# A two-layer graph network kernel on one core: how the border rows of its scatter stage are made, and when half 1 of its source-ordered groups runs

## The chip, the cores and the metric

The kernel is one program on one core of a Trainium2 chip. Its time is the device time of that core in microseconds (us); the median of three timed runs stands for it. PE is TensorE, DVE VectorE, ACT ScalarE, POOL GpSimd and SP SyncE, which here only issues DMAs.

## What is computed

Two graph layers over 6,250 nodes. Layer 0 has 100,000 edges, 16 attributes for each, and takes a maximum over the edges of each node; `row` is `src`, and the edges come sorted by `dst`:

```python
def _L0_gnn_ref(x, edge_attr, row, col, W_m1, b_m1, ...):
    msg_1 = x @ W_m1.T + b_m1               # 6250 x 96
    msg_2 = x @ W_m2.T + b_m2
    msg_e = edge_attr @ W_me.T + b_me       # one row for each edge
    msg = jax.nn.relu(msg_1[row] + msg_2[col] + msg_e)
    msg = jax.nn.relu(msg @ W_net.T + b_net)
    agg = jax.ops.segment_max(msg, row, num_segments=N_NODES)
    agg = jnp.where(jnp.isfinite(agg), agg, 0.0)
    out = x @ W_o1.T + b_o1 + (agg @ W_o2.T + b_o2)
    return out
...
    x = _layernorm(x + _L0_gnn_ref(x, edge_attr_16, src, dst, ...), axis=-1)
    x = _layernorm(x + _L1_gnn_ref(x, edge_attr_16, src, dst, ...), axis=-1)
```

Layer 1 is an edge network of two dense layers with a GELU over the same edges, a sum over them for each node, and a norm. The change leaves it as it is; it takes the second half of the time.

## The kernel before, in words

Nodes are cut in 49 blocks of 128 (`NB`) for `src` and in 56 blocks of 112 (`ND`) for `dst`. Edges are handled in groups of four chunks of 128.

**Block 1** (L582 to L783) ranks the edges by `src`: 49 groups of one-hot rows on DVE (`hist_onehots`) that PE sums up (`hist_counts`), `ranks_pe` and `ranks_dve` behind them. Beside them PE makes two tables from `x1T`, the transposed nodes: `m1` (for `src`, kept as three bf16 limbs: L751, `rest` L765, and ACT's copies L679) and `m2` (for `dst`, L756 and L687).

**Block 3** (L1227 on) starts with a prologue. Where a block of 112 nodes begins inside a chunk, its row has to be made of two blocks: `border_rows` (DVE L1403), `border_turn` (PE L1622), ACT's copy (L1761), and `later_block` (PE L1615, DVE L1411) form the table `more`, four blocks (a quad) at a time, 14 quads. All engines wait for its last row (`x_chain`). SP clears 16 pad blocks of `slots` and POOL 33 meanwhile.

Then come 200 steps (`C_STEPS`) with 196 groups in `dst` order, called "c": PE turns one-hot rows and counts (`turn`, `equal`, `count`), and `product` forms four chunks in PSUM (`ps_u`), out of `dstT` times `m2` (L1567) plus the row of `more` through a product with the identity (L1571). ACT copies the sum into `ring_u` (`rows`, L1698), DVE puts each edge's place in the order of `src` in `ring_p` (`put`, L1371; `advance`, L1337, is the running count before it), and POOL scatters each chunk with one indirect DMA (L1298), four for a group. It waits for `ring_p` and `ring_u`.

The groups in `src` order, called "d", are 222: 111 (`GS`) of half 1 and 111 of half 2. One takes `load_u` on SP, `pre_u` (L1582, L1590) and `net` (L1599) on PE, `first` (L1720) on ACT, `scan` (L1395) on DVE, `turn_top` (L1607) on PE, `rows_out_of` and `store` on ACT (L1726, L1730). From step 110 (`K0`) one d turn stands in each c step, 90 in all. The other 21 turns of half 1 and half 2 follow in a `pipeline` after the c steps; half 2's loads wait until all groups have landed (`groups_sent`). The turns up to 90 (`KS`) have one PSUM bank of each kind ("alone"), the later ones two. POOL, after its last scatter, loads `x1T` again (L1303), because `ring_u` lay over its place, waits for the stores of half 1 and issues 49 gathers (L1309), later 49 for half 2 (L1316).

The order inside a step is fixed by lists named `order`, one for each engine, with a lag for each stage; `hooks` are small works tied to a step (histogram groups `H8`, `MARKS`, `RANKS`, `TABLES`).

## Time and profile before

| | us |
|---|---|
| median of three runs | 3780.2 |
| the three runs | 3772.44, 3780.2, 3789.65 |
| the profiled execution | 3754.61 |
| its span | 3752.6 |
| busy: PE, DVE, ACT, POOL | 2743.1, 1925.6, 1120.7, 1692.6 |
| granted clock of PE, mean | 0.804 of full speed |

The span is cut in stretches by what runs: to 89.4 blocks 1 and 2, to 128 the prologue, to 966 steps with c alone, to 1660 steps with c and d, to 1816 the rest of half 1, the start of half 2 and the first gathers, to 2096 half 2; layer 1 follows. `issue` as a releaser means that the engine waited for nothing that the profile shows, `remote` that the semaphore of another engine came, with a long way between its event and the start. A group or line of the kernel is named by L and its number.

### The profile page before, as it was taken

The numbers are of one execution on the slowest core, as the hardware profiler recorded it, in microseconds if no ns is written. First come the engines' busy times: TensorE is split into PE (matmuls) and PEld (weight loads), VectorE is DVE, ScalarE is ACT, GpSimd is POOL, SyncE is SP. The second block draws the span as 40 slices with busy tenths as digits, with TensorE's granted clock in tenths as the row PEclk, the third lists the DMA queues.
The fourth block names the chain that finished last, engine by engine and source line by source line (L and its number), as shares of the span: only waits on it lengthen the run. The fifth ranks groups of instructions, "written<-read, shape, count | busy, mean of one in ns | idle before, by whom it ended". The sixth has DMA issues, their size and how long they took to land. (4 is left out here: it accounts for less than half of the span.)

```text
span 3752.6 us, 82895 instructions
## 1 busy us (share of the span) xinstructions
PE 2743.1 (73%) x22172; PEld 2390.7 (64%) x22173; DVE 1925.6 (51%) x8319; ACT 1120.7 (30%) x2463; POOL 1692.6 (45%) x1819
## 2 busy tenths in 40 slices
PE   7877777776888878886699756666666666676667
PEld 6766666666776667764466545665666666666667
DVE  6644544433555555555588733444444444444446
ACT  3222222222344444444466621111111111111114
POOL 1455544555545454443311135555455454545443
PEclk8677767777899999888799877777777777777778
DMA  6322223111333333356588311111111111111111
GB/s 190 79 72 71 71 70 87 37 40 33 84 97 96 93 92 97 92 153 159 142 201 200 85 41 38 36 36 37 34 36 36 35 38 35 36 34 37 34 33 35
DMA packets 575909, 276.48 MB, mean 74 GB/s; under 512 B 499504, under 2 KB 542826, under 8 KB 575546
## 3 DMA queue, kind: packets, MB, share of 16 engines
q1 hardware_dynamic: 225752, 107.85, 11.9%
q0 software_dynamic: 55104, 99.54, 9.7%
q10 hardware_dynamic: 294818, 66.10, 8.4%
q8 instruction: 129, 2.11, 0.2%
q14 instruction: 106, 0.87, 0.1%
HBM read 151.69 MB, written 127.59 MB: 74 GB/s over the span
## 5 line engine op out<-in xcount | busy, mean ns | idle before, releaser
L1298 POOL DMA_INDIRECT edge_in_src_order<-ring_u,ring_p x784 | 772.1, 985 | 782.1 <-issue 493.0
L1979 POOL DMA_INDIRECT a_rows<-src_table,idx x782 | 744.0, 951 | 744.4 <-DMA idx<-src_c 521.2
L2059 PE MATMUL ps_h<-a_rows,ident 128*128 x1664 | 325.8, 327 | 276.4 <-issue 275.7
L2059 PEld LDWEIGHTS ps_h<-a_rows,ident 128*128 128x128 f32 x1664 | 276.6, 235 | 311.3 <-issue 310.8
L2099 ACT ACTIVATE h<-ps_h 128x512 f32<-128x512 f32 x208 | 124.2, 597 | 1151.8 <-remote 812.3
L2028 DVE TENSOR_SCALAR ohd_f<-iota_b,dloc_c 128x128 f32<-128x128 bf16 x832 | 186.0, 292 | 509.9 <-remote 424.8
L2064 PE MATMUL ps_h<-bpart,dstT_b 128*128 x1664 | 317.2, 351 | 171.5 <-ACT dstT_b L2093 137.0
L2064 PEld LDWEIGHTS ps_h<-bpart,dstT_b 128*128 128x128 f32 x1664 | 278.1, 253 | 202.0 <-issue 201.8
L1395 DVE TENSOR_TENSOR_SCAN top<-same,top,bank 96x512 f32<-96x512 bf16 x221 | 281.6, 1274 | 174.5 <-remote 109.0
L1337 DVE TENSOR_TENSOR prior<-bank,earlier 128x512 f16<-128x512 f32 x196 | 134.8, 688 | 454.6 <-remote 369.1
L2016 DVE TENSOR_TENSOR hsumT<-hsumT,ps_s 128x128 f32 x832 | 239.3, 288 | 191.1 <-issue 83.5
L1567 PEld LDWEIGHTS bank<-m,dstT 128*128 128x128 f32 x1568 | 240.8, 226 | 98.8 <-issue 96.7
L1599 PE MATMUL bank<-msg,wnet_s 97*96 97x512 f32 x444 | 252.8, 649 | 67.6 <-issue 41.3
L2073 PE MATMUL ps_s<-ohd_f,h 128*128 128x128 f32 x1664 | 283.2, 325 | 19.8 <-issue 14.6
L1567 PE MATMUL bank<-m,dstT 128*128 x1568 | 259.3, 313 | 35.5 <-issue 25.3
L2073 PEld LDWEIGHTS ps_s<-ohd_f,h 128*128 128x128 f32 x1664 | 266.5, 242 | 22.8 <-issue 18.8
L1571 PE MATMUL bank<-more,ident 128*128 x1568 | 251.5, 309 | 15.4 <-issue 13.2
L1571 PEld LDWEIGHTS bank<-more,ident 128*128 128x128 f32 x1568 | 227.9, 222 | 24.8 <-issue 22.9
L1590 PE MATMUL bank<-oh_b,m_s 128*96 128x128 bf16 x2664 | 203.7, 227 | 44.5 <-issue 37.6
L1720 ACT ACTIVATE msg<-bank,bias_c 96x512 f32<-96x512 f32 x222 | 151.2, 681 | 251.6 <-remote 235.6
L1590 PEld LDWEIGHTS bank<-oh_b,m_s 128*96 128x96 bf16 x2664 | 188.8, 129 | 48.2 <-issue 39.8
L1714 ACT COPY m_s<-m 128x288 bf16 x444 | 169.8, 430 | 159.7 <-PE bank L1590 104.2
(347 smaller groups left out, 5104.4 us busy)
## 6 DMA issues: line engine op xcount, KB each, us to landing
u_in<-edge_in_src_order SPq DMA_DIRECT2D x222, 192.0 KB
running_max<-row ACTq DMA_DIRECT2D x222, 192.0 KB
rowt<-src_row SPq DMA_DIRECT2D x222, 130.0 KB
running_max<-zero_rows ACTq DMA_DIRECT2D x37, 576.0 KB
key_b<-dst_of_edges ACTq DMA_DIRECT2D x832, 0.5 KB
edge_in_src_order<-ring_u,ring_p POOLq DMA_INDIRECT x784
a_rows<-src_table,idx POOLq DMA_INDIRECT x782
dge_attributes_by_column<-in_edge_attrT SPq DMA_DIRECT2D x8, 784.0 KB, 12.1
```

Source lines behind the costliest of these rows:

```text
L1298: pool.indirect_dma_start(u_d, bass.IndirectOffsetOnAxis(ring_p[:, j:j + 1], 0), ring_u[:, j, :], None).then_inc(sent[i % 4], 16)
L1395: v.tensor_tensor_scan(top[:, u % 2, :], same[:, u, :], pick_bank(ps_net, i, u), 0.0 if first else top[:, (u - 1) % 2, 4 * P - 1:4 * P], A ...
L1567: m.matmul(ps_u[:, j, :], dstT[:, u, j, :], m2[:, bass.ds(at[j], F)], start=(j == 0), stop=False, skip_group_check=True)
L1571: mm = m.matmul(ps_u[:, j, :], ident[:], more[:, bass.ds(of[j], F)], start=False, stop=True, skip_group_check=True)
L1590: mm = m.matmul(to[:, P * j:P * j + P], m1_s[:, u % 2, j, F * k:F * k + F], oh[:, u % 2, P * j:P * j + P], start=False, stop=(k == 2), ski ...
L1599: m.matmul(pick_bank(ps_net, i, u), wnet_s[:], msg[:, u % 2, :], start=True, stop=True).then_inc(net_ready, 1)
L1979: pool.indirect_dma_start(a_rows[:, 4 * u + j, :], None, a_d, bass.IndirectOffsetOnAxis(idx[:, u % 4, j:j + 1], 0)).then_inc(got[u % 4], 16)
L2016: adds.add(v.tensor_tensor(at, at, ps_s[k][:, j, :], ALU.add))
L2028: last = v.tensor_scalar(ohd[:, u, j, :], iota_b[:], dloc[:, u, j:j + 1], None, ALU.is_equal)
L2059: m.matmul(ps_h[k][:, j, :], ident[:], a_rows[:].rearrange("p c d -> p (c d)")[:, bass.ds(slot[j], D)], start=(j == 0), stop=False, skip_g ...
L2064: mm = m.matmul(ps_h[k][:, j, :], dstT[:, k, j, :], bpart[:, bass.ds(at[j], D)], start=False, stop=True, skip_group_check=True)
L2073: mm = m.matmul(ps_s[k][:, j, :], h[:, u, j, :], ohd[:, u, j, :], start=True, stop=True)
```

## The change

- `x1T` gets a place of its own, so the ten DMAs of L1303 are gone. The index inputs of block 1 lie in `agg_all` instead.
- Block 1 no longer makes `m1`. It makes the border rows instead: DVE `border_dve`, PE `border_pick`, DVE `border_local`, and then 14 quads of `border_rows`, of which POOL takes nine (36 instructions) and DVE five (19), with `border_turn` on PE and `border_copy` on ACT. PE waits for all of these copies before `ranks_pe`.
- Block 3 has no prologue. The quads' products and joins (`border_product`, `border_join`) stand in the hooks of steps 0, 1 and 2 (5, 5 and 4 quads); the histogram groups start one step later; `m1` is made in the hooks of steps 7 to 36 through PSUM bank 6.
- In `product` the four products with the identity are gone. ACT writes the rows of `more` into `ps_u` first (`seed`, lag 2, between `rows` and `rows_out_of`), and PE's four products add to them. `product` waits for `seeded`, and `seed` for `u_ready`.
- SP clears 20 pad blocks and POOL 29.
- All 111 turns of half 1 stand in the 90 steps from `K0` on (`in_turns`): 21 steps have a second d turn, behind everything else of the step. `KS` is 112. SP waits for `groups_sent` and then the 111 turns of half 2 follow.

```diff
+                def turn_of_half_1(now):
+                    return max(0, now - K0) * GS // (C_STEPS - K0)
+                def in_turns(order, now):
+                    ds = range(turn_of_half_1(now), turn_of_half_1(now + 1))
+                    for kind, lag, work in order:
+                        if kind == "c":
+                            step([(kind, lag, work)], "c", CG, now)
+                        elif ds:
+                            step([(kind, lag, work)], "d", GB, ds[0])
+                    for t in ds[1:]:
+                        for kind, lag, work in order:
+                            step([(kind, lag, work)], "d", GB, t)
...
-                KS = C_STEPS - K0 + 1 & -2
+                KS = GS + 1 & -2
...
                         def product(i, u, n):
                             pe.wait_ge(rec_in[u], 16 * (n + 1))
-                            wait(pe, u_ready, i)
+                            pe.wait_ge(seeded, i + 2)
                             at = offsets(nc, mybir.EngineType.PE, pf_row[:, 4 * i:4 * i + 4], ND * F - F)
                             for j in range(4):
-                                m.matmul(ps_u[:, j, :], dstT[:, u, j, :], m2[:, bass.ds(at[j], F)],
-                                         start=(j == 0), stop=False, skip_group_check=True)
-                            of = offsets(nc, mybir.EngineType.PE, xs_row[:, 4 * i:4 * i + 4], ND * F - F)
-                            for j in range(4):
-                                mm = m.matmul(ps_u[:, j, :], ident[:], more[:, bass.ds(of[j], F)],
-                                              start=False, stop=True, skip_group_check=True)
+                                mm = m.matmul(ps_u[:, j, :], dstT[:, u, j, :], m2[:, bass.ds(at[j], F)],
+                                              start=False, stop=(j == 3), skip_group_check=True)
                             mm.then_inc(sum_ready, 1)
...
+                        def seed(i, u, n):
+                            act.wait_ge(x_chain, ND)
+                            act.wait_ge(seeded, i + 1)
+                            wait(act, u_ready, i)
+                            at = offsets(nc, mybir.EngineType.Activation, xs_row[:, 4 * i:4 * i + 4], ND * F - F)
+                            for j in range(4):
+                                last = s.copy(ps_u[:, j, :], more[:, bass.ds(at[j], F)])
+                            last.then_inc(seeded, 1)
...
-                        for lo in range(0, NP, 5 * P):
-                            hi = min(lo + 5 * P, NP)
-                            g.dma_start(x1T[:, lo:hi], xT[:, lo:hi]).then_inc(x_back, 16)
```

On PE, in a step with one c group and one d turn near the middle of the stage, the c part of before stands so (`bank<-m,dstT` is L1567, `bank<-more,ident` L1571; `TENSOR_LOAD` and `ISA` fetch the four offsets):

```order
3822 L79 TENSOR_LOAD rows_b
3823 L1567 ISA
3824 L1567 MATMUL bank<-m,dstT 128x96
...
3830 L1567 MATMUL bank<-m,dstT 128x96
3831 L79 TENSOR_LOAD rows_b
3832 L1571 ISA
3833 L1571 MATMUL bank<-more,ident 128x96
...
3839 L1571 MATMUL bank<-more,ident 128x96
3840 L1536 MATMUL bank<-ohlo_a,prior 128x64 x4
```

And so after the change, on PE in a step with two d turns; L1632 is `net`, L1640 `turn_top`, L1615 and L1623 `pre_u`, L1566 the last of `equal`:

```order
3281 L1632 MATMUL bank<-msg,wnet_s 96x512
3282 L79 TENSOR_LOAD rows_b
...
3290 L1604 MATMUL bank<-m,dstT 128x96
3291 L1640 MATMUL bank<-ident,top 128x96 x4
3292 L1573 MATMUL bank<-ohlo_a,prior 128x64 x4
...
3300 L1566 MATMUL bank<-hiT 128x128 x4
3301 L1615 MATMUL bank<-ident,u_in 96x128 x4
3302 L1623 MATMUL bank<-oh_b,m_s 96x128 x12
3303 L1632 MATMUL bank<-msg,wnet_s 96x512
3304 L1640 MATMUL bank<-ident,top 128x96 x4
3305 L1615 MATMUL bank<-ident,u_in 96x128 x4
3306 L1623 MATMUL bank<-oh_b,m_s 96x128 x12
```

The identity products are gone, and `net`, `turn_top` and `pre_u` of the second turn stand in a row behind the step.

On ACT, in a step with one d turn, before:

```order
711 L1708 CAST dstT<-bank 112x512
712 L1698 COPY ring_u<-bank 128x384
713 L1726 COPY row<-bank 128x384
714 L1730 DMA running_max<-row 128x4x96
```

and after:

```order
1858 L1758 CAST dstT<-bank 112x512
1859 L1748 COPY ring_u<-bank 128x384
1860 L79 TENSOR_LOAD rows_b
1861 L1735 ISA
1862 L1735 COPY bank<-more 128x96
...
1868 L1735 COPY bank<-more 128x96
1869 L1776 COPY row<-bank 128x384
1870 L1780 DMA running_max<-row 128x4x96
```

`seed` (L1735) stands between the copy of the finished sum and the copy of the d turn's rows.

On DVE, in a step with two d turns, after the change (L1428 is `put`, L1452 `scan`, L1394 `advance`, which before stood right behind the one scan and L1355):

```order
2802 L1428 SCALAR_TENSOR_TENSOR ring_p<-across,spare 128x4
...
2813 L1452 SCALAR_TENSOR_TENSOR top<-same,top,bank 96x512
2814 L1441 TENSOR_SCALAR oh_b<-rowt,node_c 128x512
2815 L1443 TENSOR_TENSOR same<-rowt 96x512
...
2821 L1452 SCALAR_TENSOR_TENSOR top<-same,top,bank 96x512
2822 L1412 TENSOR_TENSOR rank_r<-rank_r,new 100x64
2823 L1394 TENSOR_TENSOR prior<-bank,earlier 128x512
```

The second turn's one-hot, copies and scan moved in ahead of the next group's `advance`.

## Rows read from the trace of the kernel before

**Rows 1.** Windows of all engines: stretch, then busy time, clock, DMA.

```profile
24.00:71.00 47.00, 47.00 (x551) 42.27 (x551) 35.97 (x94) 22.12 (x40) 0.00 (x0) 0.95 0.89 243
89.40:128.00 38.60, 34.84 (x179) 33.27 (x179) 27.82 (x120) 8.10 (x14) 18.23 (x34) 0.50 0.26 64
128.00:970.00 842.00, 622.57 (x5830) 544.31 (x5830) 386.79 (x2163) 218.40 (x471) 432.32 (x439) 0.77 0.25 63
970.00:1660.00 690.00, 563.48 (x5808) 477.94 (x5807) 391.83 (x1774) 299.12 (x670) 335.93 (x341) 0.90 0.36 95
1750.00:1816.00 66.00, 10.26 (x46) 5.96 (x44) 4.87 (x11) 2.82 (x6) 43.52 (x47) 0.54 0.21 47
```

The columns are the stretch, its length, then busy time and records of PE, PEld (weight load), DVE, ACT and POOL, and last the granted clock, the DMA share and GB/s.

**Rows 2.** The page's costliest groups: scatters and the two products.

```profile
L1298 POOL DMA_INDIRECT edge_in_src_order<-ring_u,ring_p x784 | 772.1, 985 | 782.1 <-issue 493.0
L1567 PE MATMUL bank<-m,dstT 128*128 x1568 | 259.3, 313 | 35.5 <-issue 25.3
L1571 PE MATMUL bank<-more,ident 128*128 x1568 | 251.5, 309 | 15.4 <-issue 13.2
```

**Rows 3.** Windows of the copy into ring_u (L1698), one per c step.

```profile
138.00:966.00 828.00, 53.25 (x110) 0.77 0.24 62
966.00:1661.00 695.00, 41.30 (x86) 0.90 0.36 95
```

**Rows 4.** Windows of the scan (L1395), one for each d turn.

```profile
966.00:1661.00 695.00, 109.01 (x86) 0.90 0.36 95
1680.00:1745.00 65.00, 31.36 (x25) 1.00 0.85 227
1745.00:1816.00 71.00, 4.56 (x5) 0.57 0.26 58
1816.00:2094.00 278.00, 130.82 (x103) 0.99 0.79 197
```

**Rows 5.** Timeline of DVE, the first and fifth scan after the c steps.

```profile
1660.20 1.28 DVE L1395 TENSOR_TENSOR_SCAN top<-same,top,bank 96x512 f32<-96x512 bf16 x1 [0.60 <-remote]
...
1677.51 1.28 DVE L1395 TENSOR_TENSOR_SCAN top<-same,top,bank 96x512 f32<-96x512 bf16 x1 [1.05 <-PE bank L1607]
```

A row of the timeline has start, duration, engine, line, operation, and in brackets the idle time before it with what released it.

**Rows 6.** Timeline around one burst of scatters, c alone: POOL, PE, ACT.

```profile
865.74 0.96 POOL L1298 DMA_INDIRECT edge_in_src_order<-ring_u,ring_p  x1 [0.31 <-issue]
870.94 0.96 POOL L1298 DMA_INDIRECT edge_in_src_order<-ring_u,ring_p  x1 [4.24 <-DVE ring_p L1371]
...
859.66 1.13 PE L1571 MATMUL bank<-more,ident 128*128 x8
870.02 1.91 PE L1571 MATMUL bank<-more,ident 128*128 x8
...
866.93 0.48 ACT L1698 COPY ring_u<-bank 128x384 f32<-128x384 f32 x1 [7.73 <-remote]
```

**Rows 7.** Timeline of one step with c and d: POOL, then DVE.

```profile
1123.74 0.96 POOL L1298 DMA_INDIRECT edge_in_src_order<-ring_u,ring_p  x1 [0.30 <-issue]
1127.27 1.07 POOL L1298 DMA_INDIRECT edge_in_src_order<-ring_u,ring_p  x1 [2.57 <-issue]
...
1124.89 0.69 DVE L1337 TENSOR_TENSOR prior<-bank,earlier 128x512 f16<-128x512 f32 x1 [2.78 <-remote]
1126.31 0.15 DVE L1371 SCALAR_TENSOR_TENSOR ring_p<-across,spare 128x4 int32<-128x4 f32 x1
```

**Rows 8.** Timeline of the prologue: a quad's products, its joins, the first scatter.

```profile
116.80 1.97 PE L1615 MATMUL bank<-m,dstT_x 112*128 112x96 f32 x8
...
123.33 1.36 DVE L1411 SCALAR_TENSOR_TENSOR more<-more,joint,bank 128x96 f32<-128x96 f32 x4 [0.42 <-PE bank L1615]
...
141.94 1.05 POOL L1298 DMA_INDIRECT edge_in_src_order<-ring_u,ring_p  x1 [28.31 <-DVE ring_p L1371]
```

**Rows 9.** Timeline of DVE in block 1, beside a cast of POOL.

```profile
12.72 0.79 DVE L431 TENSOR_SCALAR cmp_r<-bounds_r,dst_f 128x128 f32<-128x128 f32 x1
```

**Rows 10.** Timeline of POOL: the first gather of half 1.

```profile
1745.27 1.00 POOL L1309 DMA_INDIRECT agg_all<-running_max,last_i  x1 [69.38 <-SPq L1252]
```

More of the change, by code:

```diff
@@ L308, in gnn @@
         rec_moved = sem(whole, "rec_moved")
-        x_back = sem(whole, "x_back")
         agg_in = [sem(whole, f"agg_in{k}") for k in range(4)]
@@ L313, in gnn @@
         wo1_set = sem(whole, "wo1_set")
+        x1T = sb(whole, "x1T", [D, NP])
         with ExitStack() as t:
@@ L664, in _ @@
                             g.tensor_copy(dst_c[:], dst_ci[:]).then_inc(dstc_set, 1)
+                            for q in range(BY):
+                                border_rows(pool, g, q, 0)
                         @block.scalar
@@ L998, in _ @@
                                 chunks_dve(dve, v, ch, k0, bank[1])
+                                border_dve(dve, v, 1, bank[1])
+                                border_local(dve, v, 1, bank[1])
+                                for q in range(BX):
+                                    border_rows(dve, v, q, 1)
                                 dve.wait_ge(k0.off_set, 2)
@@ L1051, in _ @@
                                 chunks_act(act, nc.scalar, k0, bank[4:6], bank[6:8])
+                                for q in range(BX):
+                                    border_copy(act, nc.scalar, q, 1, bank[2:4])
                                 ranks_act(act, nc.scalar, c0, 0, bank[3])
@@ L1506, in _ @@
                         for now in range(C_STEPS):
-                            for kind, lag, work in order:
-                                step([(kind, lag, work)], kind, CG if kind == "c" else GB, now - (0 if kind == "c" else K0))
+                            in_turns(order, now)
                             hooks(now)
-                        pipeline(dve, GB, [(lag, work) for kind, lag, work in order if kind == "d"], done=C_STEPS - K0, early=KS + 4)
+                        pipeline(dve, GB, [(lag, work) for kind, lag, work in order if kind == "d"], done=GS, early=KS + 4)
                         groups_sent(dve, CG)
@@ L1754, in hooks @@
                             if now == K0 - 1:
+                                act.wait_ge(m_taken, 3 * NT)
                                 act.wait_ge(apart, 1)
-                        order = [("d", 2, first), ("c", 1, turned), ("c", 3, rows), ("d", 5, rows_out_of), ("d", 6, store), ("d", 0, stage)]
-                        for q in range(BX):
-                            act.wait_ge(x_turned, q + 1)
-                            wait(act, x_ready, q - 1)
-                            k = min(4, ND - 1 - 4 * q)
-                            s.copy(dstT_x[:, q % 2, 0:k].rearrange("p j e -> p (j e)"), ps_split[q % 2][0:BD, 0:P * k]).then_inc(x_copied, 1)
-                        act.wait_ge(x_chain, ND)
+                        order = [("d", 2, first), ("c", 1, turned), ("c", 3, rows), ("c", 2, seed), ("d", 5, rows_out_of), ("d", 6, store), ("d", 0, stage)]
                         for now in range(C_STEPS):
-                            for kind, lag, work in order:
-                                step([(kind, lag, work)], kind, CG if kind == "c" else GB, now - (0 if kind == "c" else K0))
+                            in_turns(order, now)
                             hooks(now)
                         act.wait_ge(rows_cleared, 16 * ZEROS)
-                        pipeline(act, GB, [(lag, work) for kind, lag, work in order if kind == "d"], done=C_STEPS - K0, early=KS + 4)
+                        pipeline(act, GB, [(lag, work) for kind, lag, work in order if kind == "d"], done=GS, early=KS + 4)
                         for k in range(4):
```

345 lines of the change are left out of this document (182 added, 163 removed).

## The prediction

> **What bounds the kernel now.** I read the windows first, then the costliest groups, then the timeline at one place of each stretch. The windows [rows 1] show PE busy for 622.57 of 842 us with c alone and for 563.48 of 690 us with c and d; POOL is at half in both. PE looks like the bound, and the change takes work from PE. The timeline says otherwise. POOL issues a scatter of 0.985 us with 0.30 between [rows 2, 6], so a group is four times 1.27, about 5.1 us. While such a burst runs, a semaphore from PE reaches the others late: the identity products started at 859.66 and took 1.13, but ACT copied their sum only at 866.93, after 7.73 us idle with releaser `remote`, just as the last scatter of the burst (865.74 + 0.96) was over [rows 6]. POOL then waited 4.24 us for `ring_p` of DVE. With c and d the same loop is regular [rows 7]: the last scatter ends at 1124.70, DVE's `advance` starts at 1124.89 after 2.78 us `remote`, `put` at 1126.31, the next group at 1127.27. That is 5.1 us of burst plus 2.57 of a chain through DVE and POOL, in which PE's products have no part. The strongest evidence is the copy into `ring_u` [rows 3]: 828 us for 110 steps is 7.53 a step with c alone; with c and d 90 steps take 695 us, 7.7 a step, though each has a whole d turn more on PE. A d turn costs PE, by half 2 where nothing else runs, about 2.5 us (257 busy in 278 us for 103 turns would be that; the 278 us themselves are 2.70 a turn [rows 4]). So 2.5 us more on PE moved the step by 0.17 to 0.2.
>
> **The change part by part**, against the profiled 3754.61 us.
>
> *Start of the scatters.* The first starts at 141.94 [rows 8]. The prologue of 38.6 us [rows 1] goes; the products of 14 quads (1.97 us each while PE is at 0.50 of its clock, the lower level of 1.2 GHz) and their joins (1.36 us) [rows 8] come back inside steps 0 to 2, and every `seed` waits for the last join. That is 14 x 1.36 = 19 us if DVE paces them, 14 x 1.97 = 28 if a cold PE does; I take 21, since the two overlap and PE comes out of less idle time. Block 1: from 24 to 71 us PE was busy for 47.00 of 47 us and DVE for 35.97 [rows 1]. Without the three limbs of `m1` DVE sets the pace, at most 11 us less, but it takes 19 row instructions and the border sums itself, and PE waits for the border copies before the ranks. I take 3.5 and keep 0 and 11. Sum: -38.5 + 21 - 3.5 = **-21**, bounds -11 and -30. POOL's share of the clears shrinks from 33 to 29 and is done before then, so it costs nothing; its cover is some 10 us thick.
>
> POOL's nine quads in block 1 run beside DVE's one-hot rows. The nearest row is a DVE instruction of 128x128 f32 beside a cast of POOL, 0.79 us [rows 9]; 36 of POOL's instructions at that length are 28 us, in some 45 us of histogram, so they are hidden at no loss. The Trainium skill, "SBUF — State Buffer", section "Who interferes with whom", speaks against this part: a DVE instruction with two inputs in SBUF, as the one-hot rows are, contends with one of GpSimd that reads SBUF, through a pair of ports that one of them holds for the whole instruction. By it the one-hot rows would wait for POOL and the 3.5 us would turn into a loss of some 3 to 10; no row of this case settles it.
>
> *Steps with c alone (110).* PE loses the identity products, 251.5 us in 196 steps [rows 2], 1.28 a step (8 records; 1.13 warm, 1.91 cold [rows 6]) and one fetch of offsets. If a step were PE's, that would be all gain: -140. If the loop of burst and late semaphore holds, the slope above, 0.2 in 2.5, gives 0.1 a step: -11. I take 0.18 a step, **-20**, because with c alone PE is cold more often and is sometimes late by itself; that is near the slope, for it is measured on the same loop. Bounds 0 and -90. ACT gets four copies a step and a fetch. One copy of all four blocks is 0.48 us [rows 6], so they cost between 0.48 and 4 x 0.48 = 1.9. ACT is busy for 218.40 of 842 us [rows 1]: hidden in time. What stands in the chain is new: `rows` then `seed` then `product`, where `product` waited for `rows` alone. The next product needs it one step later, and a step is 7.5 us against 2.4, so no one waits for it.
>
> *Steps with c and d (90).* The same products and copies, at the slope: 90 x 0.08 = **-7**, bounds +20 and -60 (ACT is busy for 299.12 of 690 [rows 1] and gets up to 171 us more, 68%). Making `m1` in the hooks puts 20 us on PE and 30 copies on ACT over 30 steps; beside a 2 us wait for the burst in each, nothing.
>
> *The second d turn in 21 steps.* It stands behind the step's other work on each engine; on DVE its scan goes ahead of the next `advance`, the instruction that releases the next burst. In one bank a turn costs 4.3 us by itself (1660.20 to 1677.51 is four turns [rows 5]). DVE waits 2.78 us for the burst anyway [rows 7], and PE 0 to 1. If all of it falls in there, the price is the slope's 0.25 a turn, +5; if nothing, 4.3, +90. I take the middle, 2.1 a turn: **+44**. The middle, because its inputs cross between PE and ACT twice, and with POOL in its burst a crossing is late, while half of its work fits.
>
> *The tail.* 21 turns no longer stand between the last scatter and the gathers. They ran at 2.6 us a turn (25 in 65 us [rows 4]), the first at 4.3; 21 x 2.7 = **-57**. What half 2 does meanwhile is not lost: from 1660 to 1745 it had begun with 8 turns, and it still has 111 to do at 2.70 [rows 4]. SP's wait for `groups_sent` now stops an empty pipeline: last landing, load, three lags, **+8**, bounds 5 and 20. The 49 gathers come 66 us of near standstill as before (PE 10.26 of 66 us [rows 1], 5 scans in 71 us [rows 4]), wherever they fall. POOL had waited 69.38 us before the first gather [rows 10], so its ten loads of `x1T` were hidden and their absence is worth 0.
>
> Sum: -21 - 20 - 7 + 44 - 57 + 8 = **-53**, so 3702 against 3754.6. The median of the shown runs is 3780.2, 25.6 above the profiled run; the prediction is 3780.2 - 53 = **3727**.
>
> **The rivals.**
> *PE is the bound after all.* For it: busy 74 and 82% [rows 1]. Against: rows 3 and 7. Half of what the product lost in 196 steps would be -125 in place of -27, so -151: 3629. All of it: 3504. Chance 0.17.
> *The second turn takes the place of DVE's slack.* Slower. If the second scan of a step starts after the burst is over, `advance`, `put` and the next burst come later by the whole turn: +90 for 44. With it the products give nothing (0 for -27) and the empty pipeline costs 20 for 8: -21 + 90 - 57 + 20 = +32, 3812. It decides from the point where a second turn's inputs arrive more than 2.8 us after the first scan. For it: the crossings. Against: rows 7, where the wait of 2.78 is longer than the scan's 1.3. Chance 0.15.
> *A colder clock.* PE's granted clock is 0.77 with c alone and 0.90 where it has more to do; it is 0.54 where it is idle [rows 1], and eight products take 1.9 us in place of 1.1 [rows 6]. With less work PE may be at 1.2 GHz more often: if one step in three that is now warm turns cold, 37 x 0.8 = +29, and the -20 is gone, -53 + 49 = -4: 3776. Chance 0.16. The Trainium skill, "TensorE: Matmul & The Clock Gate", section "HAM oscillation — how this bites in real kernels", says that gaps between bursts of matmuls put the clock back to half, each time anew. The trace agrees (0.77 in a stretch full of gaps); the page would give this rival, since the gaps grow by what the product loses.
>
> **How the numbers follow.** The sum has 0.52, the others as above. Its own range is 3680 to 3765 by the bounds of the double steps and of the c steps. The range of 8 in 10 leaves out the far end of the first rival (about 0.1) and the slower rival's far end (0.08): 3645 to 3795. A measurement of this kernel tells about 0.5% from no change, 19 us. Faster by more: 0.50 of the sum, all of the first rival, little of the clock: 0.68. Within: 0.17, mostly the clock. Slower: 0.15.
>
> **What would show it.** The first scatter near 121 us; a c step at 7.35 us and a c and d step at 7.6, with double steps near 9.8 (the copies into `ring_u` in windows); `advance` still released by `remote` at the end of a burst; the first gather at 1745.27 - 21 - 20 - 7 + 44 - 57 + 8, near 1692 us, with some 8 turns of half 2 before it, and half 2 at 2.70 a turn. I am wrong if the c step falls below 7 us (PE was the bound), if double steps take over 12 us, if the first scatter comes after 130, or if the granted clock with c alone is under 0.7.

## The result and the profile after

The changed kernel takes 3732.4 us (median of four runs, 3724.6 to 3745.5) and the kernel before 3779.0 us (four runs, 3772.4 to 3789.7): a ratio of 0.9883, 95% interval 0.9857 to 0.9908. The forecast was 3727.

The windows of the changed kernel, with the same columns as [rows 1]: block 1, the start of block 3, c alone, c and d, the first gathers, half 2.

```profile
24.00:71.00 47.00, 43.17 (x505) 37.94 (x505) 42.44 (x117) 13.30 (x24) 33.56 (x36) 1.00 0.94 260
...
86.00:124.00 38.00, 30.44 (x205) 28.50 (x206) 27.38 (x100) 6.59 (x19) 16.04 (x30) 0.63 0.44 101
124.00:960.00 836.00, 549.13 (x4957) 463.94 (x4955) 376.24 (x2120) 306.96 (x924) 431.11 (x440) 0.70 0.24 61
960.00:1684.00 724.00, 552.75 (x5589) 448.56 (x5590) 432.23 (x1874) 396.03 (x1092) 345.25 (x340) 0.87 0.40 105
...
1710.00:1800.00 90.00, 32.05 (x233) 22.57 (x231) 23.95 (x52) 18.35 (x41) 48.33 (x51) 0.64 0.37 88
1800.00:2072.00 272.00, 249.22 (x2171) 180.19 (x2170) 220.46 (x489) 174.75 (x395) 44.63 (x47) 1.00 0.80 196
```

With c alone PE is busy for 549 of 836 us, where it was 623 of 842 [rows 1], and its granted clock is 0.70 instead of 0.77. ACT has gone from 218 to 307 us. The stretch has not become shorter. That is best seen at the copies into `ring_u`: their 1st, 110th, 111th and last in the changed kernel, and then the same four in the kernel before.

```profile
120.77 0.48 ACT L1748 COPY ring_u<-bank 128x384 f32<-128x384 f32 x1 [1.24 <-PE bank L1604]
...
953.07 0.50 ACT L1748 COPY ring_u<-bank 128x384 f32<-128x384 f32 x1
959.33 0.48 ACT L1748 COPY ring_u<-bank 128x384 f32<-128x384 f32 x1 [1.12 <-remote]
...
1683.97 0.48 ACT L1748 COPY ring_u<-bank 128x384 f32<-128x384 f32 x1 [6.47 <-remote]
```

```profile
138.69 0.48 ACT L1698 COPY ring_u<-bank 128x384 f32<-128x384 f32 x1 [2.04 <-PE bank L1571]
...
960.91 0.48 ACT L1698 COPY ring_u<-bank 128x384 f32<-128x384 f32 x1 [1.81 <-PE bank L1571]
967.14 0.49 ACT L1698 COPY ring_u<-bank 128x384 f32<-128x384 f32 x1
...
1659.97 0.48 ACT L1698 COPY ring_u<-bank 128x384 f32<-128x384 f32 x1 [0.91 <-remote]
```

So the start is 17.9 us earlier; 109 steps with c alone take 832.3 us for 822.2, 10.1 longer; 85 steps with c and d take 724.6 for 692.8, 31.8 longer, with 20-odd second turns in them. What comes after that is shorter: half 2's last two scans (one row of the view) start 386.4 us behind the last copy, where they started 432.9 behind it. These four add up to -22.5 us, and the spans differ by 20.6 (3732.0 and 3752.6). The medians differ by 46.6, because the profiled run of before was 24 us under its median; so no single stretch of this pair may be read closer than some 20 us.

The experiments ran on four chips, and the table below can't be read without that. On two (here A1 and A2) the kernel before takes 3727 us, 1.4% under the recorded 3779; on two others (B1, B2) the same program takes 2661 and 2663 us. Each chip was used in one session only, so what is called a kind of chip below may also be a state in which the chips were found.

### The profile page after: what moved, and what is told of

Same layout as the page of the kernel before. It is cut to its first block and busy times, and to the rows that moved or that the text cites. A ratio compares the mean times of both kernels' runs of the same rounds, so it can differ in the third digit from the quotient of the medians.

```text
span 3732.0 us, 80433 instructions
## 1 busy us (share of the span) xinstructions
PE 2598.2 (70%) x20605; PEld 2232.4 (60%) x20606; DVE 1919.0 (51%) x8284; ACT 1261.5 (34%) x3246; POOL 1721.3 (46%) x1841
## 5 line engine op out<-in xcount | busy, mean ns | idle before, releaser
L1359 POOL DMA_INDIRECT edge_in_src_order<-ring_u,ring_p x784 | 780.2, 995 | 800.6 <-issue 549.2
L2105 PEld LDWEIGHTS ps_h<-a_rows,ident 128*128 128x128 f32 x1664 | 278.4, 237 | 324.8 <-issue 324.0
L1452 DVE TENSOR_TENSOR_SCAN top<-same,top,bank 96x512 f32<-96x512 bf16 x221 | 281.0, 1272 | 147.0 <-remote 88.7
L1604 PEld LDWEIGHTS bank<-m,dstT 128*128 128x128 f32 x1568 | 263.9, 244 | 148.8 <-issue 147.7
L1604 PE MATMUL bank<-m,dstT 128*128 x1568 | 283.1, 332 | 76.1 <-issue 57.2
L1394 DVE TENSOR_TENSOR prior<-bank,earlier 128x512 f16<-128x512 f32 x196 | 134.7, 687 | 377.6 <-remote 340.5
L1632 PE MATMUL bank<-msg,wnet_s 97*96 97x512 f32 x444 | 266.3, 680 | 71.7 <-DVE top L1452 35.8
L1623 PE MATMUL bank<-oh_b,m_s 128*96 128x128 bf16 x2664 | 210.6, 229 | 67.7 <-issue 67.6
L1623 PEld LDWEIGHTS bank<-oh_b,m_s 128*96 128x96 bf16 x2664 | 192.6, 131 | 77.8 <-issue 76.4
L1770 ACT ACTIVATE msg<-bank,bias_c 96x512 f32<-96x512 f32 x222 | 151.0, 680 | 160.7 <-remote 122.9
L1735 ACT COPY bank<-more 128x96 f32 x784 | 148.8, 237 | 129.7 <-ACT ring_u L1748 83.7
L1615 PE MATMUL bank<-ident,u_in 128*96 128x128 f32 x888 | 144.4, 286 | 41.6 <-ACT msg L1770 34.3
```

The source lines that it names most:

```text
L1359: pool.indirect_dma_start(u_d, bass.IndirectOffsetOnAxis(ring_p[:, j:j + 1], 0), ring_u[:, j, :], None).then_inc(sent[i % 4], 16)
L1452: v.tensor_tensor_scan(top[:, u % 2, :], same[:, u, :], pick_bank(ps_net, i, u), 0.0 if first else top[:, (u - 1) % 2, 4 * P - 1:4 * P], A ...
L1604: mm = m.matmul(ps_u[:, j, :], dstT[:, u, j, :], m2[:, bass.ds(at[j], F)], start=False, stop=(j == 3), skip_group_check=True)
L1623: mm = m.matmul(to[:, P * j:P * j + P], m1_s[:, u % 2, j, F * k:F * k + F], oh[:, u % 2, P * j:P * j + P], start=False, stop=(k == 2), ski ...
L1632: m.matmul(pick_bank(ps_net, i, u), wnet_s[:], msg[:, u % 2, :], start=True, stop=True).then_inc(net_ready, 1)
L2105: m.matmul(ps_h[k][:, j, :], ident[:], a_rows[:].rearrange("p c d -> p (c d)")[:, bass.ds(slot[j], D)], start=(j == 0), stop=False, skip_g ...
```

## The experiments

Every kernel here, the controls too, waits in three places of the gathers and of layer 1 against a loaded value masked with `& 255`, which changes none of the values. All edits are against the changed kernel, but for r1. "Against before" is the ratio to the kernel before on the same chip. The stretches are from the profiled run, as the copies into `ring_u` mark them. The code of the c steps is the same in the recorded changed kernel, r3 and e5, and with c alone in e2 too: their stretches lie between 810.0 and 832.3 us with c alone and between 707.1 and 724.6 with c and d, which shows how closely one trace may be read.

| run | chip | median us | against before (95%) | 1st copy at | c alone, 109 steps | c and d, 85 steps | last copy to half 2's last two scans |
|---|---|---|---|---|---|---|---|
| before (recorded) | - | 3779.0 | 1 | 138.7 | 822.2 | 692.8 | 432.9 |
| after (recorded) | - | 3732.4 | 0.9883 (0.9857 to 0.9908) | 120.8 | 832.3 | 724.6 | 386.4 |
| r3 after | A2 | 3689.3 | 0.9909 (0.9884 to 0.9935) | 123.1 | 813.8 | 719.1 | 383.4 |
| e8 products back | A2 | 3723.4 | 0.9996 (0.9973 to 1.0019) | 120.2 | 817.7 | 748.5 | 384.2 |
| e3 longer burst | A2 | 3532.3, one run | - | 120.6 | 712.9 | 661.6 | 387.4 |
| e6 split burst | A2 | 3633.0, one run | - | 120.6 | 771.3 | 700.2 | 389.3 |
| e2 one turn a step | A1 | 3682.1 | 0.9874 (0.9852 to 0.9897) | 120.5 | 817.2 | 658.7 | 436.8 |
| e5 gathers in pairs | A1 | 3626.4 | 0.9731 (0.9709 to 0.9753) | 120.5 | 810.0 | 707.1 | 322.9 |
| r1 before | B1 | 2662.4, one run | - | 138.5 | 524.0 | 466.1 | 373.6 |
| r2 after | B1 | 2659.7 | 0.9994 (0.9980 to 1.0009) | 121.9 | 524.1 | 536.6 | 324.8 |
| e1 products back | B1 | 2643.6 | 0.9934 (0.9918 to 0.9951) | 120.1 | 525.9 | 514.3 | 326.6 |
| e4 no border rows | B1 | 2605.3 | 0.9786 (0.9770 to 0.9802) | 120.5 | 523.5 | 450.4 | 354.7 |
| c1 pairs, DMA in mid | B2 | 2824.2 | 1.0608 (1.0590 to 1.0627) | 120.9 | 557.9 | 526.8 | 336.6 |
| c2 pairs, DMA at end | B2 | 3250.2 | 1.2211 (1.2191 to 1.2232) | 120.0 | 555.7 | 535.6 | 327.4 |

**The kernel before, once more.**

> The kernel before once more, for a second trace of it. The profiled run of before (3754.6 us) lay 24 us under the median of its timed runs (3779.0), while that of after (3733.8) lay on its own (3732.4). If that was chance, this trace shows a time near 3779, and the 20 to 25 us sit in the c steps (the copies into ring_u took 822.2 us from the first to the 110th, and 692.8 from the 111th to the last); the start (138.7), the tail and layer 1 should repeat within 3 us. If timed runs are always slower than a profiled one, this trace repeats 3755 within 5.

It ran on a chip of the second kind, and neither expectation fits: 2662 us. With that it became the most telling of all runs, since the kernel is the same. What DVE waited for in the steps with c alone (line and operand, releaser, us in total, times, longest), first in the recorded trace from 200 to 900 us, then here from 200 to 600:

```profile
DVE prior L1337 <- remote: 185.8, 34, 9.2
DVE prior L1337 <- PE bank L1529: 64.8, 18, 6.8
```

```profile
DVE prior L1337 <- PE bank L1529: 60.9, 58, 4.4
```

In the recorded trace 31 of these 34 releases come during the last scatter of a run or up to 1.9 us behind it. (`remote` has to be read with care: the semaphore's event stands right before the start, and what is long is the way to it from the end of PE's instruction. In [rows 6] the products ended at 860.79 and the copy began at 866.93.) On B1 the late semaphores are gone, and POOL goes from group to group without a break, here over a border of two groups:

```profile
602.28 0.96 POOL L1298 DMA_INDIRECT edge_in_src_order<-ring_u,ring_p  x1 [0.31 <-issue]
603.54 0.96 POOL L1298 DMA_INDIRECT edge_in_src_order<-ring_u,ring_p  x1 [0.30 <-issue]
604.80 0.95 POOL L1298 DMA_INDIRECT edge_in_src_order<-ring_u,ring_p  x1 [0.30 <-DMA edge_in_src_order<-ring_u,ring_p]
```

POOL's waits before a scatter, for `ring_p` in the recorded trace (150 to 1665 us) and the most frequent here (150 to 1154 us), where none is longer than 0.3 us:

```profile
POOL edge_in_src_order L1298 <- DVE ring_p L1371: 259.3, 56, 7.5
```

```profile
POOL edge_in_src_order L1298 <- issue: 208.9, 685, 0.3
```

A scatter takes what it takes on the first kind (0.96 and 0.30 between). From the first scatter of the 1st group to that of the 111th a group takes 5.17 us (141.7 to 710.9) for 7.56 in the recorded trace (141.9 to 973.5). The copies would say 524.0 / 109 = 4.81, but on B1 they run up to some eight groups ahead of the scatters (the 111th copy is at 667.7). So on the first kind of chip some 2.4 us of each step, a third, is the stop that the prediction read out of [rows 6, 7]; the reading is confirmed, but for one kind of chip, which the trace of before alone could not show.

With c and d on B1 it is PE that sets the pace of the copies, 5.48 us a step, while POOL lives on its lead. The columns are those of [rows 1]:

```profile
668.00:1134.00 466.00, 466.00 (x5828) 423.17 (x5825) 396.39 (x1776) 292.74 (x673) 356.19 (x361) 1.00 0.54 143
```

Half 2 behind a burst of gathers shows the stop of the first kind again: scans (L1395) in the 62 us of the burst of 49 here, and then (L1452) in the 62 us of the recorded changed kernel; the columns are those of [rows 4].

```profile
1218.00:1280.00 62.00, 28.37 (x23) 1.00 0.96 224
```

```profile
1720.00:1782.00 62.00, 4.89 (x4) 0.60 0.33 75
```

**The changed kernel, twice more.**

> The changed kernel once more, control for the experiments of this call. Expected 3732 us within 10. From the trace: first copy into ring_u at 120.8, 832.3 us to the 110th copy, 724.6 from the 111th to the last, within 10 us each; granted clock with c alone 0.70.

> The changed kernel again, control of this call, since the chips differ (c step 7.6 us in the recorded traces, 4.8 on one chip). On a chip of the recorded kind: about 1.2% under the kernel before. On the other kind: no difference.

The first expectation missed by a thousand us, because the run fell on B1; there the change is worth nothing (0.9994). On A2 it is worth 0.9%, as the recorded pair says within the intervals. Its clock with c alone was 0.71 on A2.

**Products back on PE, no copies on ACT.**

```diff
                         def product(i, u, n):
                             pe.wait_ge(rec_in[u], 16 * (n + 1))
-                            pe.wait_ge(seeded, i + 2)
+                            pe.wait_ge(x_chain, ND)
+                            wait(pe, u_ready, i)
...
+                            of = offsets(nc, mybir.EngineType.PE, xs_row[:, 4 * i:4 * i + 4], ND * F - F)
+                            for j in range(4):
+                                mm = m.matmul(ps_u[:, j, :], ident[:], more[:, bass.ds(of[j], F)],
+                                              start=False, stop=True, skip_group_check=True)
...
-                        order = [("d", 2, first), ("c", 1, turned), ("c", 3, rows), ("c", 2, seed), ("d", 5, rows_out_of), ("d", 6, store), ("d", 0, stage)]
+                        order = [("d", 2, first), ("c", 1, turned), ("c", 3, rows), ("d", 5, rows_out_of), ("d", 6, store), ("d", 0, stage)]
```

> The changed kernel with the four identity products of each group back on PE and no copies on ACT; all else as after. Theory 1 (a c step is a burst of scatters plus a chain behind it in which PE's work has little part): the stretch with c alone and that with c and d stay within 10 us of the changed kernel's, total within 15. Theory 2 (PE's work sets the step): 196 x 1.3 = +250 us, half of it at least +125. Theory 3 (ACT's four copies stand in the chain that ends last, or a colder clock ate the gain): faster than the changed kernel by 10 to 40 us, with the granted clock back at 0.77 with c alone.

> The changed kernel with the identity products back on PE and no copies on ACT, a second time, for a chip of the recorded kind. Theory 1 (the step is a burst plus a chain in which the products have little part): within 15 us of the control, where 250 us of PE work come back; with the granted clock with c alone back from 0.70 to 0.77. Theory 2 (PE's work paces): +125 to +250. Theory 3 (copies on ACT in the chain): 10 to 30 us faster. On the other kind of chip it repeats its 16 us (0.6%) under the control.

On A2 the move from PE to ACT is worth 34 us by the medians (3723.4 against 3689.3; the two intervals don't touch). The copies of the two traces put 3.9 of it in 109 steps with c alone and 29.4 in 85 with c and d. That the two add up to the medians' difference is luck: the spans of these traces differ by 18.9 only (3719.2 and 3700.3), since r3's first copy is 2.9 us late, the step between its 110th and 111th copy takes 12.8 us for 6.3, and the part behind half 2 takes 5.8 more. By the spread of the same code above, the 3.9 can't be told from nothing, and the 29.4 is good to some 15. PE's windows on A2, 140 to 950 and 960 to 1660 us, first with the copies on ACT and then with the products back:

```profile
140.00:950.00 810.00, 533.52 (x4815) 452.37 (x4815) 366.38 (x2074) 302.55 (x906) 423.88 (x432) 0.71 0.24 62
960.00:1660.00 700.00, 548.60 (x5477) 447.43 (x5475) 424.86 (x1843) 388.98 (x1069) 331.33 (x331) 0.86 0.39 106
```

```profile
140.00:950.00 810.00, 620.10 (x5730) 538.76 (x5729) 369.05 (x2089) 225.04 (x482) 423.84 (x431) 0.77 0.25 63
960.00:1660.00 700.00, 574.45 (x5906) 487.32 (x5905) 411.72 (x1758) 317.75 (x710) 319.59 (x320) 0.90 0.38 101
```

87 us of PE work with c alone bought nothing that can be told: there theory 1 holds. For the whole kernel no theory does, since 34 us are over theory 1's 15 and far under theory 2's 125. The granted clock fell from 0.77 to 0.71 as PE did less, so the mechanism of the clock rival is there too; what it cost isn't told apart.

On B1, where POOL sets the pace with c alone, the products cost nothing there either (525.9 and 524.1), and with c and d the move costs 22 us (16 in the whole kernel: what theory 3 expected). With the products, first here, PE is almost never idle; with the copies it has 44 us less to do and waits for ACT instead.

```profile
651.00:1165.00 514.00, 513.46 (x6272) 459.16 (x6272) 441.39 (x1876) 329.16 (x752) 363.37 (x370) 1.00 0.57 151
```

```profile
651.00:1188.00 537.00, 469.65 (x5593) 390.55 (x5592) 439.23 (x1877) 384.59 (x1095) 363.03 (x370) 0.97 0.54 144
```

```profile
PE bank L1615 <- ACT msg L1770: 30.9, 21, 1.7
PE bank L1640 <- ACT row L1776: 21.5, 19, 1.5
PE bank L1604 <- ACT bank L1735: 8.5, 13, 0.8
```

So ACT, busy for 385 of 537 us, is late with its own work for the d turns (`first`, L1770, and `rows_out_of`, L1776), and less so with the copies themselves (L1735).

**Neither products nor copies.**

> The changed kernel without any border rows in the product: neither the copies on ACT nor the products on PE, so the sums of edges in a border chunk are wrong; the table itself is still made and waited for. It tells the cost of the copies (against the changed kernel) from that of the products (against the kernel with the products back). Theory 1: all three within 15 us of each other. Theory 3 with ACT: this one is faster than the changed kernel by 10 to 40 us and as fast as, or faster than, the one with products. Clock theory: it is no faster than the changed kernel and its clock is as low (0.70), while the one with products is faster than both.

It leaves out the rows of the second block in a border chunk. On B1 the kernel takes 2605.3 us without them, 38 less than with the products and 54 less than with the copies, so theory 1 failed on this chip and theory 3 was right in its direction. The clock theory failed too: this kernel is the fastest of the three with a granted clock of 0.85 with c alone, under the 0.88 and 0.93 of the others. The copies into `ring_u` put the difference in the steps with c and d: 450.4 us without, 514.3 with products, 536.6 with copies, or 0.75 and 1.01 us a step. Part of that is only lead over POOL, which never stops in this run (5.15 us a group): the last scatter comes at 1135.8, 1174.3 and 1197.2, or 0.45 and 0.72 us a step. With c alone all three are the same, 523.5 to 525.9.

**One d turn a step.**

```diff
                 def turn_of_half_1(now):
-                    return max(0, now - K0) * GS // (C_STEPS - K0)
+                    return max(0, now - K0)
...
-                KS = GS + 1 & -2
+                KS = C_STEPS - K0 + 1 & -2
```

with the 21 turns and SP's wait behind the c steps as before.

> The changed kernel with one d turn in each of the last 90 steps, as before, and the other 21 turns of half 1 behind the c steps; all else as after. The spreading alone is then this run against the changed kernel. The chip matters: where a burst of scatters holds back the others' semaphores (the recorded pair of traces, c step 7.6 us), the sum of the prediction says that spreading costs 21 x 2.1 = 44 in the steps with c and d and gives 57 back less 8: this run within 10 us of the changed kernel. Where POOL issues without a break (the last call's chip, c step 4.8 us), the copies into ring_u from the 111th to the last took 466 us before, 537 after, and the stretch behind them 374 and 325; with the copies of the border rows alone I expect some 22 us of the 71: 485 to 495 here, the stretch behind at 374: total within 10 us of the changed kernel's 2660. The rival, that spreading is pure gain, puts this run 40 or more above the changed kernel.

Against e5 on the same chip, whose c steps are those of the changed kernel, the steps with c and d take 658.7 for 707.1 us: the 21 second turns cost 48.4, 2.3 each. But the profiled run of e5 (3605.5) was 21 us under its median; against the 719.1 of r3 and the 724.6 of the recorded trace, on other chips, they cost 60 and 66, up to 3.1 each. On B1 the kernel before and the one with the products back differ by 48.2 (466.1 and 514.3); PE is busy all the time in both, so there the 2.3 us are PE's own work for a turn. Behind the c steps one turn a step costs 436.8 against 386.4 and 383.4, 50 to 53 us. By the medians e2 stands to before as the changed kernel does (0.9874 and 0.9883, 0.9909, with intervals that overlap): the spreading gives back what it takes, to some 15 us. Its edit ran on A1 alone; on B1 the same follows from before and e1, 48.2 more in the steps and 47.0 less behind them.

**Gathers in pairs.**

```diff
-                        for b in range(NB):
-                            wait(pool, agg_in[b % 4], 16 * (b // 4))
-                            pool.indirect_dma_start(agg_all[:, b, :], None, s_d, ...
                         for b in range(NB):
                             at = offsets(nc, mybir.EngineType.Pool, need_row[:, b:b + 1], GB)
                             pool.wait_ge(stored, at[0])
...
+                            wait(pool, agg_in[b % 4], 16 * (b // 4))
+                            pool.indirect_dma_start(agg_all[:, b, :], None, s_d, ...
```

> The changed kernel with each of the 49 gathers of half 1 issued right before the gather of half 2 of the same block, in place of a burst of 49 ahead of them. Theory (a burst of POOL's indirect DMAs holds back the semaphores of the others, so that half 2 all but stops for 60 us): where the c step is 7.6 us, half 2 goes on from the start, with 3 scans in the 60 us of the burst replaced by some 22; gain 30 to 60 us. Where the burst holds nothing back (22 scans during the 61 us of the burst in each trace of the last call), the gain is under 10 us, or the end comes later by a few us because gathers queue at the end. Rival for the first kind of chip (the gathers' traffic slows the turns, not their issue): no gain on either, or a loss of 10 to 20.

The pairs, and the scans (L1451) of half 2 in the first 62 us of them:

```profile
1684.09 0.96 POOL L1373 DMA_INDIRECT m<-running_max,last_i  x1 [0.30 <-issue]
1687.29 0.94 POOL L1370 DMA_INDIRECT agg_all<-running_max,last_i  x1 [2.24 <-SPq L1314]
1688.53 1.06 POOL L1373 DMA_INDIRECT m<-running_max,last_i  x1 [0.30 <-issue]
```

```profile
1683.00:1745.00 62.00, 28.00 (x22) 1.00 0.88 212
```

22 turns where the burst let 4 pass, and the stretch behind the c steps is 322.9 us for 386.4, 63 less; so the rival, that the gathers' traffic slows the turns, falls. The kernel is 2.7% under the kernel before, where the changed kernel is 0.9 to 1.2% under it. On B2 the same pairs stand in c1 and c2, and that stretch is 336.6 and 327.4 for 324.8 with the burst: nothing to gain there.

**A longer burst.**

```diff
                                 pool.indirect_dma_start(u_d, ...).then_inc(sent[i % 4], 16)
+                            if i >= 44:
+                                pool.wait_ge(rest_set, 16 * (NB - 20) + 32 * (i - 44))
+                                for k in range(2):
+                                    g.dma_start(wm[:, F * k:F * k + F], xT[:, F * k:F * k + F]).then_inc(rest_set, 16)
```

> The changed kernel with two more plain DMAs of POOL behind the four scatters of each group from group 44 on (152 groups), some 1.2 us of POOL's time a group; nothing waits for their data. Theory 1: every us of the burst is a us of the step: +1.2 x 152 = +180 us, of which 80 in the stretch with c alone (66 groups) and 100 with c and d. Theory 2 (PE paces, POOL has 2.5 us of slack in a step): under +40. On the other kind of chip, where POOL issues without a break with c alone, +80 there and less with c and d.

Both expectations failed, and not by a little: 1.2 us more for POOL in each group made the kernel 157 us faster than r3 on the same chip (3532, one run, and 3689). From the 45th group to the 111th a group takes 6.67 us for 7.64, and POOL mostly issues without a break:

```profile
802.64 0.96 POOL L1359 DMA_INDIRECT edge_in_src_order<-ring_u,ring_p  x1 [0.30 <-issue]
803.60 1.16 POOL L1364 DMA_DIRECT2D wm<-in_xT  x2
805.07 1.01 POOL L1359 DMA_INDIRECT edge_in_src_order<-ring_u,ring_p  x1 [0.30 <-issue]
806.38 0.99 POOL L1359 DMA_INDIRECT edge_in_src_order<-ring_u,ring_p  x1 [0.30 <-issue]
```

and DVE's waits for `remote` from 450 to 900 us, r3 first, shrink:

```profile
DVE prior L1394 <- remote: 112.6, 14, 9.0
```

```profile
DVE prior L1398 <- remote: 65.0, 21, 4.0
```

14 of these 21 releases come while a plain DMA runs; of r3's 14 all came 1.0 to 1.8 us behind the last scatter of a run. So what holds the others back on this kind of chip is not the length of POOL's burst; it fits the rows that a plain DMA after each four scatters lets the semaphores through. That is one run, and why a plain DMA would do so isn't shown.

**A split burst.**

```diff
                             for j in range(4 * (i % RG), 4 * (i % RG) + 4):
+                                if i >= 44 and j % 4 == 2:
+                                    for k in range(2):
+                                        wait(pool, idle_set, 2 * (i - 44) + k)
+                                        g.memset(wm[:], 0.0).then_inc(idle_set, 1)
                                 pool.indirect_dma_start(u_d, ...
```

> The changed kernel with two small memsets of POOL (each after a wait for the one before, some 0.6 us together) between the second and third scatter of each group from group 44 on. If the others' semaphores are held back only while scatters follow each other within 0.3 us, the pause lets them through in mid-burst, advance and the copy start 2.5 us earlier and a step loses up to 2 us though the burst is 0.6 longer: -100 to -250 over 152 groups. If they are held back until the queue behind POOL has drained, the pause only adds its length: +60 to +100. On the other kind of chip: +0.6 a step with c alone, +40.

The pause is 0.60 us, and c alone takes 771.3 us for 813.8, c and d 700.2 for 719.1: one run, 56 us faster than r3, between the two ranges expected. POOL still stops, by 1.88 us here:

```profile
804.04 0.60 POOL L1363 MEMSET wm<- 128x192 f32 x2
804.80 0.96 POOL L1364 DMA_INDIRECT edge_in_src_order<-ring_u,ring_p  x1 [0.16 <-issue]
806.07 0.96 POOL L1364 DMA_INDIRECT edge_in_src_order<-ring_u,ring_p  x1 [0.30 <-issue]
808.91 0.96 POOL L1364 DMA_INDIRECT edge_in_src_order<-ring_u,ring_p  x1 [1.88 <-issue]
```

And DVE's waits did not shrink with c alone. From 450 to 900 us, to compare with r3's 112.6 above:

```profile
DVE prior L1399 <- remote: 125.6, 19, 9.7
```

With c and d they did, 36.8 us (920 to 1600) for 104.7 (970 to 1660). So a pause of memsets does not do what the plain DMAs did, and where the 42 us with c alone come from stays open.

**Both at once, and in layer 1.** The gathers in pairs, one plain DMA in each group of scatters from 44 on, and one in each group of layer 1's gathers, after the second (c1) or the fourth (c2) of four.

> A version from what the experiments showed: the changed kernel with the gathers in pairs (63 us less behind the c steps), with one plain DMA of POOL (0.6 us, its data unused) after the second of the four scatters of each group from group 44 on, and the same after the second of the four gathers of each of layer 1's groups. Theory as mended by the run with the longer burst (a plain DMA between scatters lets the others' semaphores through, so that POOL goes on without a break): from group 44 a step takes 5.7 us with c alone where it took 7.5, 60 us less with c and d; if layer 1's 1648 us behind half 2 hold the same stops (on the chip without them it takes 1148), they fall by up to 500 - 196 x 0.6 = 380. Sum on a chip of the recorded kind: 3700 - 110 - 60 - 63 = 3467 if layer 1 gives nothing, 3087 if all. Rival (what helped there was that two DMAs at the end hold the next burst off): the c steps gain under 40 us. On the other kind of chip: slower than the changed kernel by 0.6 x 66 to 0.6 x 350, 40 to 200 us.

> The same with the plain DMA after the fourth scatter or gather of each group, not after the second. If any place in the stream of indirect DMAs does, it equals the one with it in the middle within 20 us. If what counts is how long indirect DMAs follow each other without another instruction (four in both), again the same. If a release near the middle of a burst is worth more, since advance and the copy into ring_u then start while the burst goes on, this one is slower by 0.5 us a step, some 75 us in the scatter steps. On a chip of the other kind both are equal.

They ran on B2, where nothing is held back, so they show only the price: 6% and 22% slower. c1 is in the range given for such a chip; c2 was expected to equal it and is 426 us slower. With c alone c1 takes 34 us more (557.9 for B1's 524.1), where 66 groups of 0.58 would be 38. In layer 1 of c2 the edit itself costs most: POOL waits for the plain DMA of the group before, right behind which the next group now stands, 454.3 us in 182 waits.

```profile
2004.57 0.59 POOL L2033 DMA_DIRECT2D wo_s<-in_xT  x1
2007.75 0.97 POOL L2030 DMA_INDIRECT a_rows<-src_table,idx  x1 [2.58 <-DMA wo_s<-in_xT]
```

What they would give on the first kind of chip wasn't measured, and neither was whether any place in the group does.

## Why the prediction was right, point by point

| term | forecast | measured |
|---|---|---|
| start of the scatters | -21 | -17.4 (first scatter 124.57 for 141.94) |
| c alone, products to copies | -20 | +10 in the recorded pair; -4 on A2, with the move alone undone; neither can be told from 0 |
| c and d, products to copies | -7 | -29 on A2, to some 15 |
| 21 second turns | +44 | +48 to +66 (e2 on A1, against e5 and two others), +48 (B1) |
| 21 turns out of the tail, less the new wait | -57 + 8 = -49 | -47 in the pair, -50 to -53 by e2 |
| sum | -53 | recorded pair: -20.6 in the spans, -46.6 in the medians; A2: -37 in the medians |

**The whole** came within 5 us, partly by luck: errors in the two kinds of c steps ran against each other, the profiled runs alone differ by 20.6 of the 53, and on the second kind of chip the same change is worth nothing. The mechanism, the loop from the end of a burst to the next one, was right for the kind of chip of the trace.

**The two terms for the d turns** are about right in size, and together they come near nothing, as forecast (44 - 49 = -5). The reason given for the first, that half of a turn fits in the wait for the burst, isn't shown: on B1 nothing fits, and a turn costs 2.3 us all the same, because that is its work on PE.

**The c steps.** The sum (-27; -33 on A2) came out by luck, since both parts missed. The step that failed is the slope. The prediction divided 695 us by 90 steps, but the stretch holds 86 copies, and 85 steps from the 111th copy to the last take 692.8: 8.15 us a step, not 7.7. A d turn then costs 0.6 us of step for 2.5 us of PE, three times the slope used, and 1.3 us less of PE would be worth 0.3 a step; measured with c and d: 29.4 / 85 = 0.35 on A2. With c alone the allowance above the slope (0.18 for 0.1) had no ground: 0.04 a step was measured. A slope from the steps with c and d says nothing of those with c alone, whose loop is not the regular one of [rows 7] either: of 66 runs of scatters between 200 and 900 us in the trace of before, 35 have four scatters and 25 have eight.

**The signs.** The c step was to fall to 7.35 us and took 7.64 (832.3 / 109), and the first gather was to come near 1692 us and came at 1720.62, late by about what the steps with c alone lacked (30). Five scans of half 2 stood before it, not eight; in the trace of before there are four, where the prediction read eight. Double steps took 10.6 us (forecast 9.8), the half 2 turn 2.74 (2.70), and the clock with c alone stood right at the limit named, 0.70.

**The clock rival** was right in its mechanism. The clock with c alone went from 0.77 to 0.70, and the mean of the product's matmuls, over all steps (L1567, [rows 2]), from 313 to 332 ns:

```profile
L1604 PE MATMUL bank<-m,dstT 128*128 x1568 | 283.1, 332 | 76.1 <-issue 57.2
```

The change still came out faster, and with c alone, where the clock fell, the stretch stayed the same within the spread. Whether the 10 us of the recorded pair are the clock or chance stays open; A2 has 0.77 and 0.71 in the same comparison and a gain of 4.

**Block 1** gave 0, not 3.5. DVE was at `dloc` at 80.56 us before and at 81.05 after. POOL took 33.56 us for its 36 rows, 0.93 each (the window above), where DVE does 19 in 4.02, and DVE waited 1.64 us for it at the end:

```profile
42.40 0.41 DVE L336 TENSOR_TENSOR ohlo<-lo_f,iota 128x512 bf16<-128x512 bf16 x1
42.74 0.63 DVE L336 TENSOR_TENSOR ohhi<-hi_f,iota 128x784 bf16<-128x784 bf16 x1
...
67.29 4.02 DVE L563 TENSOR_SCALAR oh_x<-iota_b,split_l 128x112 f16<-128x112 bf16 x19 [1.64 <-POOL oh_x L563]
```

The row of 0.79 us taken for POOL's length ([rows 9]) was DVE's own and too short. DVE's larger one-hot (`ohhi`) took 0.55 to 0.63 us beside POOL and 0.55 to 0.56 without, the smaller (`ohlo`) 0.41 to 0.50 and 0.41 to 0.43. The Trainium skill, "SBUF — State Buffer", section "Who interferes with whom", has such instructions contend; the trace agrees in direction, by at most 0.08 us an instruction, not by the 0.93 us of POOL's.

**The PE-bound rival** fell on the kind of chip of the trace: 250 us of products are worth 34 on A2. On B1 with c and d it describes the kernel before (PE busy for 466.00 of 466 us); what PE was spared there it lost again to waits for ACT. **The slower rival** fell: the second turn cost 2.3 to 3.1, not 4.3.

**What no rival had** is the chip. On the second kind POOL is the pace with c alone and PE with c and d, the stop of 2.4 us a step doesn't exist, and the change is 0.9994.

## What to carry to other kernels

A busy share of 74% on one engine said nothing here; the loop from the last scatter of a burst to the first of the next did, and it told in advance that 250 us of matmuls would be worth some 30. Count the steps of a stretch by its records before dividing, and measure a slope in the stretch where it will be used. Moving a turn from behind a loop into its steps pays only if it costs less there (2.3 to 3.1 us) than outside (2.4), which here it didn't. Moving work from a busy engine to an idle-looking one can lose on both: the idle-looking one may be in the chain of other work. A burst of POOL's indirect DMAs was better spread among the work of the others on the first kind of chip. And one trace of one chip can show a stop that other chips don't have.

## What the runs showed of the hardware

- Same program, two kinds of chip (or of state): 3727 and 2661 us. On the first, semaphores of PE reach DVE and ACT late beside runs of indirect DMAs on POOL, most of them as the run ends or up to 1.9 us behind it (`remote`, up to 9.2 us at `advance`); on the second no such wait is in the trace. Layer 1 behind half 2, which gathers in the same way, takes 1650 us on the first and 1150 on the second. Why is open.
- On the first kind, two plain DMAs (1.16 us) after each four indirect ones made the kernel 157 us faster, and two memsets (0.60 us) in their middle 56 us; each is from one run of the edit, and only with the plain DMAs did the waits for late semaphores shrink with c alone. On the second kind such DMAs cost what they take.
- Four copies of ACT out of SBUF with an offset each, 236 ns each, cost more than the eight-record product on PE that they replace: 54 and 38 us in the whole kernel on B1.
